# A mixture-of-experts kernel: turns of the next expert's first rows moved from the closing down products into the last block's up products

## The chip, the cores and the metric

The kernel runs on one core of a Trainium2 chip. The metric is the device time of one execution in microseconds (us). The time before is the median of 3 runs.

## The reference

The input x is two sequences of 2048 rows of 512 numbers (4096 tokens). It goes through a gated cross attention (16 heads, keys and values from a context of 128 rows each) and then through a gated mixture of experts, which is the stage that the change touches:

```python
xf = layernorm(x).reshape(4096, 512)
top_v, top_i = top_k(xf @ router_w.T, 2)          # two of 8 experts per token
C = ceil(4096 * 2 * 1.25 / 8)                     # 1280 slots per expert
slot = where(pos < C, experts * C + pos, E * C)   # each token's place with its expert
xb = buf.at[slot].set(xf[tokens])[:E * C].reshape(8, C, 512)
g, u = split(einsum('ecd,efd->ecf', xb, w12), 2)  # d_ff 2048
yb = einsum('ecf,edf->ecd', silu(g) * u, w3)
out = zeros.at[tokens].add(yb[slot] * weights)
x = x + tanh(g_ffn) * out
```

## The kernel before, in words

The first stage (up to about 540 us of the span) does attention, layer norm and routing, and writes each token's row to its slot in a DRAM buffer, `expert_rows`. The second stage goes over the 8 experts, one after the other, in a loop of its own on each engine (`experts`, L1240 to L1287).

**Tiles and blocks.** An expert has up to 10 tiles of 128 slots. How many it needs (nt) is read from the counts at run time, and the program has one body of code for each nt from 3 to 10. `pick` (L1268) compares and branches (L1273) to the body, and L1263 goes back to the top of the loop. `BLOCKS` cuts the tiles into blocks: 10 is (4, 3, 3), 9 is (3, 3, 3), 7 is (4, 3), 5 is (3, 2), 3 is (3,). In this data the experts have 9, 10, 10, 7, 10, 9, 5 and 3 tiles, called e0 to e7 below.

**Chunks.** The hidden width of 2048 is cut into 8 chunks of 256. For a chunk, each block is taken in turn: two steps j, each with a gate product G (bank `GB`) and an up product U (bank `UB`), each of 12 matmuls (4 pieces of the depth, and 3 passes for high and low parts of a split fp32 value, `passes`, L1536 to L1542). ScalarE takes silu of G (L1404), VectorE multiplies with U into `h32` (L1500), ScalarE rounds it to `h_hi` (L1410), and VectorE makes `h_lo` (L1506). The down products (`g2`, L1604) run one block behind: 6 matmuls of 512 columns for each tile, added into `yacc` by VectorE (`add`, L1466 to L1481). Beside these, each chunk splits the next chunk's weights in 6 units: `w_high` on ScalarE (L1368) and `w_low` on VectorE (L1443).

**Turns.** The rows of an expert arrive with the slots in the partitions and must be turned. A turn (`turn`, L1544) is 4 transposes by TensorE into one of the two banks `XBK`, then a copy of the high part by ScalarE (`x_high`, L1370 to L1373, tile `slotsT_hi`) and a subtraction by VectorE (`x_low`, L1446 to L1450, tile `slotsT_lo`). The two banks take turns, so that turn i waits for `x_low` of turn i - 2. The first `XA` = 4 tiles of an expert are turned at the end of the expert before it, and the others during its own first chunk (`slots_at`).

**The closing.** In an expert's last chunk the down products of the last two blocks are not followed by another block of the expert. They run in an order written out by `closing` (L1218), which all three engines follow: turn 0, turn 1, y0, y1, turn 2, y2, turn 3, y3 and the rest, where y is a down product. Their results go to the banks that `closing_bank` names. A down product on a `YB` bank that was used before in the same closing waits until that bank's result has been added (L1648). After the closing ScalarE has also scaled each tile (`scaled`, L1392) for the scatter by GpSimd.

```python
order, downs = [("x", 0), ("x", 1)], len(closing_downs(nt))
for i in range(downs):
    order.append(("y", i))
    if 1 <= i <= XA - 2:
        order.append(("x", i + 1))
```

Each engine works through its instructions in the order written. Nothing is reordered by a scheduler, so the place of a call in this code is its place in the engine's queue.

Of the kernel before, what the change touches and what calls it, by code (L numbers as in the profile page):

```python
# [5 lines left out]
def flamingo_gated_layer(  # L6
# [64 lines left out]
    with ExitStack() as whole:  # L71
# [1046 lines left out]
        with ExitStack() as stage:  # L1118
# [94 lines left out]
            def closing_bank(nt, i):  # L1213

                from_end = len(closing_downs(nt)) - 1 - i
                return [UB[1], GB[1], UB[0], GB[0], YB[1], YB[0], YB[1], YB[0]][from_end]

            def closing(nt):  # L1218


                order, downs = [("x", 0), ("x", 1)], len(closing_downs(nt))
                for i in range(downs):
                    order.append(("y", i))
                    if 1 <= i <= XA - 2:
                        order.append(("x", i + 1))
                return order

            def by_tiles(eng, n_e, body):
                def pick(sizes):
# [63 lines left out]
            with nc.Block(no_gpsimd_drain=True) as block:  # L1293
# [71 lines left out]
                def _(act):  # L1365
# [4 lines left out]
                    def x_high(i, tp, at, done):  # L1370
                        act.wait_ge(tp, at)
                        nc.scalar.copy(xT_hi[:, :, i * P:(i + 1) * P],  # L1372
                                       XBK[i % 2][:, :].rearrange("p (k t) -> p k t", k=KD)).then_inc(done, 1)  # L1373
# [6 lines left out]
                    def chunk(nt, e, c, par, half, first, last):  # L1380
                        base, tiles = steps_before(e, c), tiles_before(e, c)
                        loads = e * (NCH // 2) + half + 1

                        def units(which):
                            for i in which:
                                if i == 0:
                                    act.wait_ge(raw_loaded[1 - par], 16 * loads)
                                if i == NU12 and not first:

                                    act.wait_ge(y_ready, tiles)  # L1390
                                w_high(1 - par, i)

                        def scaled(t):

                            act.wait_ge(y_added, downs_done(nt, tiles, t))
                            nc.scalar.activation(yout[:, t, :], yacc[:, t, :], ACT.Copy,  # L1396
                                                 scale=wslot[:, t:t + 1]).then_inc(yout_ready, tile_of(nt, t))

                        for b, width in enumerate(BLOCKS[nt]):
                            W = width * P  # L1400
                            for j in range(NJ):
                                q = NJ * b + j
                                act.wait_ge(g_ready, base + q + 1)
                                nc.scalar.activation(silu[q % 2][:, 0:W], GB[q % 2][:, 0:W], ACT.Silu)\  # L1404
                                  .then_inc(silu_ready, step_of(nt, q))
                                if first:
                                    for i in slots_at(nt, q, 0):
                                        x_high(i, xb_tp, XB * e + i - XA + 1, xb_hi)
                                act.wait_ge(h32_ready, base + q + 1)
                                nc.scalar.copy(h_hi[h_buf(nt, par, b)][:, j, 0:W], h32[q % 2][:, 0:W])\  # L1410
                                  .then_inc(hhi_ready, step_of(nt, q))
                                if first:
                                    for i in slots_at(nt, q, 1):
                                        x_high(i, xb_tp, XB * e + i - XA + 1, xb_hi)
                                units(units_at(nt, q))
                            if last and b == 0:
                                act.wait_ge(weights_ready, e + 1)
                                act.wait_ge(yout_free, e + 1)
                            if last and 0 < b < len(BLOCKS[nt]) - 1:
                                for t in block_tiles(nt, b - 1):  # L1420
                                    scaled(t)
                        if not last:
                            units(late_units(nt))
                        if first and nt < NT:
                            act.sem_inc(xb_tp, min(XB, NT - nt))
                        if last:
                            for kind, i in closing(nt):
                                if kind == "x":
                                    x_high(i, xa_tp, XA * (e + 1) + i + 1, xa_hi)
                                    continue  # L1430
                                t, earlier = closing_downs(nt)[i]
                                if not earlier:
                                    scaled(t)
                            units(late_units(nt))
# [4 lines left out]
                def _(dve):  # L1439
# [17 lines left out]
                    def chunk(nt, e, c, par, half, first, last):  # L1457
# [25 lines left out]
                        for b, width in enumerate(BLOCKS[nt]):  # L1483
# [9 lines left out]
                            for j in range(NJ):  # L1493
                                q = NJ * b + j
                                if first:
                                    for i in slots_at(nt, q, 0):
                                        x_low(i, xb_hi, XB * e + i - XA + 1, xb_lo)
                                dve.wait_ge(silu_ready, base + q + 1)
                                dve.wait_ge(u_ready, base + q + 1)
                                nc.vector.tensor_tensor(h32[q % 2][:, 0:W], silu[q % 2][:, 0:W], UB[q % 2][:, 0:W], ALU.mult)\  # L1500
# [8 lines left out]
                                if first:  # L1509
                                    for i in slots_at(nt, q, 1):  # L1510
                                        x_low(i, xb_hi, XB * e + i - XA + 1, xb_lo)
                                units(units_at(nt, q))
                            for t in downs[1:]:
                                add(t, at, opens)
# [20 lines left out]
                def _(pe):  # L1535
# [22 lines left out]
                    def chunk(nt, e, c, par, half, first, last):  # L1558
# [3 lines left out]
                        def rest_of_slots(q, half_of):  # L1562
                            for i in slots_at(nt, q, half_of):
# [3 lines left out]
                                    pe.wait_ge(xb_lo, XB * e + i - XA - 1)  # L1567
                                turn(i, xb_tp)

                        def g1(b):  # L1570
                            W = BLOCKS[nt][b] * P
                            cols = slice(first_tile(nt, b) * P, first_tile(nt, b + 1) * P)
# [9 lines left out]
                            for j in range(NJ):  # L1582
# [8 lines left out]
                                passes(GB[q % 2][:, 0:W], list(zip(stat(j), moving))).then_inc(g_ready, step_of(nt, q))  # L1591
                                if first:
                                    rest_of_slots(q, 0)
                                if q >= 2:
                                    pe.wait_ge(h32_ready, base + q - 1)
                                elif not first:
                                    pe.wait_ge(h32_ready, base)
                                else:
                                    pe.wait_ge(y_added, Y0 + tiles - 2 + 2 * q)
                                passes(UB[q % 2][:, 0:W], list(zip(stat(NJ + j), moving))).then_inc(u_ready, step_of(nt, q))  # L1600
                                if first:
                                    rest_of_slots(q, 1)

                        def g2(t, b, earlier, y=None):  # L1604

# [27 lines left out]
                        if last:  # L1633
                            downs = closing_downs(nt)
                            banks = [closing_bank(nt, i) for i in range(len(downs))]
                            for kind, i in closing(nt):
                                if kind == "x":
                                    if i % 2 == 0:
                                        pe.wait_ge(xrow_loaded[i // 2], 16 * (e + 2))
                                    if i >= 2:  # L1640
                                        pe.wait_ge(xa_lo, XA * (e + 1) + i - 1)
                                    turn(i, xa_tp)
                                    continue
                                t, earlier = downs[i]
                                at = tiles_before(e, c - 1) if earlier else tiles
# [52 lines left out]
```

## Time and profile before

| | |
|---|---|
| median of 3 runs | 2720.58 us (2719.67 to 2720.8) |
| the profiled execution | 2716.51 us |
| its span | 2714.1 us |
| TensorE busy | 2608.7 us, 96% of the span |
| VectorE busy | 1392.1 us, 51% |
| ScalarE busy | 944.7 us, 35% |
| GpSimd busy | 410.9 us, 15% |
| mean granted TensorE clock | 0.984 |

The profiled execution's own time is its span and 2.4 us around it. In the rows, PE is TensorE (PEld its weight loads), DVE is VectorE, ACT is ScalarE, POOL is GpSimd and SP is the engine that issues the loads; a q behind an engine's name is its sequencer. A matmul's recorded length is longer than the distance to the next one, because matmuls overlap, so the distance between starts is what a matmul costs. Expert e1 begins at about 856 us, e2 at 1195, e3 at 1535, e4 at 1773, e5 at 2110, e6 at 2418 and e7 at 2593.

### The profile page before, as it was taken

How to read it: one execution, taken by the hardware profiler on the slowest of the kernel's cores; microseconds unless marked ns; L12 is line 12 of the kernel's file. 1: busy time of each engine (PE TensorE's matmuls, PEld its weight loads, DVE VectorE, ACT ScalarE, POOL GpSimd, SP SyncE). 2: the span in 40 equal slices, each digit the busy share in tenths (PEclk: the TensorE clock that was granted, in tenths of full speed). 3: DMA queues.
4: the chain of work that ended last, by engine and by line, in shares of the span. 5: the costliest groups of instructions: out<-in, count | busy, mean ns of one | idle time of the engine just before them, and what ended most of it. 6: DMA issues, size and time to landing. Idle time of an engine off the chain costs nothing.

```text
span 2714.1 us, 40566 instructions
## 1 busy us (share of the span) xinstructions
PE 2608.7 (96%) x14166; PEld 2313.9 (85%) x14167; DVE 1392.1 (51%) x2647; ACT 944.7 (35%) x2479; POOL 410.9 (15%) x391
## 2 busy tenths in 40 slices
PE   5999999589999999999999999999999999999988
PEld 4877777489998888888988888888889999989987
DVE  4788888544444444444444444444444444445555
ACT  4766666222224222242222322232222322233343
POOL 2455555400002000020000300010000100030030
PEclk8999999799999999999999999999999999999999
DMA  7523222321103201132011321141011311033142
GB/s 266 213 78 102 94 78 97 122 111 47 46 27 77 86 24 46 47 62 86 23 46 46 63 109 46 47 113 40 30 46 39 107 47 46 33 85 118 70 126 81
DMA packets 60034, 208.38 MB, mean 77 GB/s; under 512 B 9564, under 2 KB 9836, under 8 KB 51602
## 3 DMA queue, kind: packets, MB, share of 16 engines
q1 hardware_dynamic: 43282, 175.30, 18.0%
q0 software_dynamic: 16640, 31.69, 6.1%
q8 instruction: 59, 0.97, 0.1%
q14 instruction: 53, 0.43, 0.1%
HBM read 145.60 MB, written 67.70 MB: 79 GB/s over the span
## 4 chain that ended last, share of the span: by engine, by line
PE 76%; issue 2%; DVE 1%; ACT 1%; DVEq 0%; DMA 0%; ACTq 0%; POOL 0%; POOLq 0%
PE bank L1540 75%; PE bank L1546 1%; DVE yacc L1480 1%; DVE slotsT_lo L1449 0%; ACT slotsT_hi L1372 0%; DVE h L1500 0%; DMA xrow<-expert_rows 0%; ACT later_hi L1368 0%; ACT yout L1396 0%; ACT h_hi L1410 0%; POOL out_dram L1354 0%; DVE w_lo L1443 0%; DVEq L1252 0%; ACT silu L1404 0%; DVEq L1479 0%
## 5 line engine op out<-in xcount | busy, mean ns | idle before, releaser
L1500 DVE TENSOR_TENSOR h<-silu,bank 128x384 f32<-128x384 f32 (+2 forms) x320 | 183.8, 574 | 826.3 <-PE bank L1540 816.8
L1540 PE MATMUL bank<-slotsT_hi,early_hi 128*128 128x384 f32 (+2 forms) x1280 | 444.6, 347 | 14.4 <-issue 12.3
L1540 PE MATMUL bank<-slotsT_hi,w_hi 128*128 128x384 f32 (+2 forms) x1280 | 442.5, 346 | 5.3 <-DVE w_lo L1443 5.3
L1540 PE MATMUL bank<-slotsT_lo,early_hi 128*128 128x384 f32 (+2 forms) x1280 | 442.5, 346 | 0.4 <-issue 0.4
L1540 PE MATMUL bank<-slotsT_lo,w_hi 128*128 128x384 f32 (+2 forms) x1280 | 442.2, 345 | 0.0
L1540 PE MATMUL bank<-slotsT_hi,early_lo 128*128 128x384 f32 (+2 forms) x1280 | 441.8, 345 | 0.0
L1540 PE MATMUL bank<-slotsT_hi,w_lo 128*128 128x384 f32 (+2 forms) x1280 | 441.1, 345 | 0.0
L1410 ACT CAST h_hi<-h 128x384 fp32r<-128x384 f32 (+2 forms) x320 | 169.2, 529 | 745.9 <-DVE h L1500 743.0
L1404 ACT ACTIVATE silu<-bank 128x384 f32<-128x384 f32 (+2 forms) x320 | 162.0, 506 | 728.8 <-PE bank L1540 728.3
L1480 DVE TENSOR_TENSOR yacc<-bank,yacc 128x512 f32<-128x512 f32 x464 | 316.6, 688 | 169.0 <-PE bank L1540 169.0
L1540 PE MATMUL bank<-later_hi,h_hi 128*128 128x512 f32 x1008 | 399.8, 397 | 0.3 <-DVE yacc L1480 0.3
L1540 PE MATMUL bank<-later_lo,h_hi 128*128 128x512 f32 x1008 | 398.7, 396 | 0.0
L1540 PE MATMUL bank<-later_hi,h_lo 128*128 128x512 f32 x1008 | 398.3, 395 | 0.0
L1354 POOL DMA_INDIRECT out_dram<-yout,token x63 | 97.9, 1554 | 1973.9 <-ACT yout L1396 1962.4
L1540 PEld LDWEIGHTS bank<-slotsT_hi,early_hi 128*128 128x128 f32 x1280 | 241.6, 189 | 30.2 <-issue 13.6
L1540 PEld LDWEIGHTS bank<-slotsT_hi,w_hi 128*128 128x128 f32 x1280 | 241.3, 189 | 20.5 <-DVE w_lo L1443 6.1
L1540 PEld LDWEIGHTS bank<-slotsT_lo,early_hi 128*128 128x128 f32 x1280 | 241.7, 189 | 13.1 <-issue 0.8
L1540 PEld LDWEIGHTS bank<-slotsT_lo,w_hi 128*128 128x128 f32 x1280 | 241.4, 189 | 12.6
L1540 PEld LDWEIGHTS bank<-slotsT_hi,early_lo 128*128 128x128 f32 x1280 | 241.6, 189 | 10.7
L1540 PEld LDWEIGHTS bank<-slotsT_hi,w_lo 128*128 128x128 f32 x1280 | 241.4, 189 | 10.8
L1506 DVE TENSOR_TENSOR h_lo<-h,h_hi 128x384 fp32r<-128x384 f32 (+2 forms) x320 | 183.8, 574 | 105.4 <-ACT h_hi L1410 104.8
L1540 PEld LDWEIGHTS bank<-later_hi,h_lo 128*128 128x128 f32 x1008 | 189.3, 188 | 44.9
(195 smaller groups left out, 3533.3 us busy)
## 6 DMA issues: line engine op xcount, KB each, us to landing
staged<-in_moe_w_dram SPq DMA_DIRECT2D x33, 1536.0 KB
raw<-in_moe_w_dram SPq DMA_DIRECT2D x32, 1536.0 KB, 6.4
xrow<-expert_rows SPq DMA_DIRECT2D x42, 520.0 KB, 9.0
expert_rows<-zeros SPq DMA_DIRECT2D x40, 520.0 KB, 7.5
xin<-in_x_dram SPq DMA_DIRECT2D x17, 512.0 KB, 3.7
xres<-in_x_dram SPq DMA_DIRECT2D x15, 512.0 KB, 3.7
out_dram<-xres SPq DMA_DIRECT2D x15, 512.0 KB
staged<-in_L_xattn_Wq_dram SPq DMA_DIRECT2D x1, 1024.0 KB, 10.7
```

The costliest lines, as they stand in the source:

```text
L1354: nc.gpsimd.indirect_dma_start(out=out_tok, out_offset=bass.IndirectOffsetOnAxis(ap=token[:, i:i + 1], axis=0), in_=yout[:, i, :] if t < n ...
L1404: nc.scalar.activation(silu[q % 2][:, 0:W], GB[q % 2][:, 0:W], ACT.Silu)\
L1410: nc.scalar.copy(h_hi[h_buf(nt, par, b)][:, j, 0:W], h32[q % 2][:, 0:W])\
L1480: nc.vector.tensor_tensor(yacc[:, t, :], y[:, :], yacc[:, t, :], ALU.add)\
L1500: nc.vector.tensor_tensor(h32[q % 2][:, 0:W], silu[q % 2][:, 0:W], UB[q % 2][:, 0:W], ALU.mult)\
L1506: nc.vector.tensor_tensor(h_lo[hb][:, j, 0:W], h32[q % 2][:, 0:W], h_hi[hb][:, j, 0:W].bitcast(fp32), ALU.subtract)\
L1540: last = nc.tensor.matmul(out_ap, st, mv, start=(at == 0), stop=(at == n - 1))
L1546: last = nc.tensor.transpose(XBK[i % 2][:, k * P:(k + 1) * P], xrow[:, i, k * P:(k + 1) * P], ident[:, :])
```

## The change

`next_slots_at` puts turn i of the next expert's first rows into the last block of the last chunk: turn 0 behind the first gate product, turn 1 behind the first up product, turn 2 behind the second gate product, turn 3 behind the second up product. A turn is only moved there when its tile of the slots' buffer belongs to an earlier block, whose products have read it by then. For nt of 7 or more all 4 turns move, for nt = 5 three of them (turn 3 stays, now ahead of the closing's first down product), and for nt = 3 none. On ScalarE and VectorE the copies and subtractions move in the same way, and `closing` keeps only what is left.

```diff
+            def next_slots_at(nt, q, half):
+                last = len(BLOCKS[nt]) - 1
+                i = 2 * (q - NJ * last) + half
+                return [i] if 0 <= i < min(XA, first_tile(nt, last)) else []
+
             def closing(nt):
-                order, downs = [("x", 0), ("x", 1)], len(closing_downs(nt))
-                for i in range(downs):
-                    order.append(("y", i))
-                    if 1 <= i <= XA - 2:
-                        order.append(("x", i + 1))
-                return order
+                turns = [("x", i) for i in range(min(XA, first_tile(nt, len(BLOCKS[nt]) - 1)), XA)]
+                downs = [("y", i) for i in range(len(closing_downs(nt)))]
+                return turns[:2] + downs[:2] + turns[2:3] + downs[2:3] + turns[3:] + downs[3:]
...
                                 nc.scalar.activation(silu[q % 2][:, 0:W], GB[q % 2][:, 0:W], ACT.Silu)\
...
+                                if last:
+                                    for i in next_slots_at(nt, q, 0):
+                                        x_high(i, xa_tp, XA * (e + 1) + i + 1, xa_hi)
                                 act.wait_ge(h32_ready, base + q + 1)
                                 nc.scalar.copy(h_hi[h_buf(nt, par, b)][:, j, 0:W], h32[q % 2][:, 0:W])\
...
+                                if last:
+                                    for i in next_slots_at(nt, q, 1):
+                                        x_high(i, xa_tp, XA * (e + 1) + i + 1, xa_hi)
                                 units(units_at(nt, q))
...
+                                if last:
+                                    for i in next_slots_at(nt, q, 0):
+                                        x_low(i, xa_hi, XA * (e + 1) + i + 1, xa_lo)
                                 dve.wait_ge(silu_ready, base + q + 1)
                                 dve.wait_ge(u_ready, base + q + 1)
...
+                                if last:
+                                    for i in next_slots_at(nt, q, 1):
+                                        x_low(i, xa_hi, XA * (e + 1) + i + 1, xa_lo)
                                 units(units_at(nt, q))
...
+                        def next_slots(i):
+                            if i % 2 == 0:
+                                pe.wait_ge(xrow_loaded[i // 2], 16 * (e + 2))
+                            if i >= 2:
+                                pe.wait_ge(xa_lo, XA * (e + 1) + i - 1)
+                            turn(i, xa_tp)
...
                                 passes(GB[q % 2][:, 0:W], list(zip(stat(j), moving))).then_inc(g_ready, step_of(nt, q))
...
+                                if last:
+                                    for i in next_slots_at(nt, q, 0):
+                                        next_slots(i)
...
                                 passes(UB[q % 2][:, 0:W], list(zip(stat(NJ + j), moving))).then_inc(u_ready, step_of(nt, q))
...
+                                if last:
+                                    for i in next_slots_at(nt, q, 1):
+                                        next_slots(i)
```

**VectorE, nt = 10, the last block of the last chunk and the start of the closing.** In these rows bank6 and bank7 are the turns' banks, h32 and h_lo belong to the block's second step, later_lo is a unit of the next weights, and yacc is an add. Before:

```order
L1500 TENSOR_TENSOR h32_1<-silu1,bank3 128x384
L1506 TENSOR_TENSOR h_lo1<-h32_1,h_hi1 128x384
L1442 REGISTER_ALU
L1443 TENSOR_TENSOR later_lo<-staged,later_hi 128x512
L1447 ISA
L1449 TENSOR_TENSOR slotsT_lo<-bank6,slotsT_hi 128x4x128
L1447 REGISTER_ALU
L1449 TENSOR_TENSOR slotsT_lo<-bank7,slotsT_hi 128x4x128
L1469 REGISTER_ALU
L1480 TENSOR_TENSOR yacc<-bank4,yacc 128x512
```

And now:

```order
L1458 TENSOR_TENSOR slotsT_lo<-bank6,slotsT_hi 128x4x128
L1510 REGISTER_ALU
L1512 TENSOR_TENSOR h32_1<-silu1,bank3 128x384
L1518 TENSOR_TENSOR h_lo1<-h32_1,h_hi1 128x384
L1456 REGISTER_ALU
L1458 TENSOR_TENSOR slotsT_lo<-bank7,slotsT_hi 128x4x128
L1451 REGISTER_ALU
L1452 TENSOR_TENSOR later_lo<-staged,later_hi 128x512
L1478 REGISTER_ALU
L1489 TENSOR_TENSOR yacc<-bank4,yacc 128x512
```

One subtraction of a turn now stands ahead of the product h32, and one between h_lo and the weights' unit. Before, two stood behind the unit and ahead of the first add.

**TensorE, nt = 10, the last up product's end and the closing's start.** xrow are the rows that are turned, and later_hi and h_hi the operands of a down product. Before, two turns stood together between the up product and y0:

```order
L1540 MATMUL bank<-slotsT_lo,w_hi 128x384
L1540 MATMUL bank<-slotsT_hi,w_lo 128x384
L1639 ISA
L1546 MATMUL bank<-ident,xrow 128x128 x8
L1653 REGISTER_ALU
L1540 MATMUL bank<-later_hi,h_hi 128x512
```

And now one turn stands there, and one behind each of the three products before it, of which this is the second gate product's:

```order
L1555 MATMUL bank<-slotsT_hi,w_lo 128x384
L1589 REGISTER_ALU
L1561 MATMUL bank<-ident,xrow 128x128 x4
L1555 MATMUL bank<-slotsT_hi,w_hi 128x384
L1555 MATMUL bank<-slotsT_lo,w_hi 128x384
```

The closing's 36 matmuls of down products now follow each other with no turn between them.

## Rows read from the trace of the kernel before

**Rows 1.** The page: span, busy time and instructions, and the chain by line

```profile
span 2714.1 us, 40566 instructions
...
PE 2608.7 (96%) x14166; PEld 2313.9 (85%) x14167; DVE 1392.1 (51%) x2647; ACT 944.7 (35%) x2479; POOL 410.9 (15%) x391
...
PE bank L1540 75%; PE bank L1546 1%; DVE yacc L1480 1%; DVE slotsT_lo L1449 0%; ACT slotsT_hi L1372 0%; DVE h L1500 0%; DMA xrow<-expert_rows 0%; ACT later_hi L1368 0%; ACT yout L1396 0%; ACT h_hi L1410 0%; POOL out_dram L1354 0%; DVE w_lo L1443 0%; DVEq L1252 0%; ACT silu L1404 0%; DVEq L1479 0%
```

**Rows 2.** Waits of TensorE from 560 us to the end: total us, times, longest

```profile
PE bank L1540 <- issue: 5.6, 3, 2.7
PE bank L1540 <- DVE w_lo L1443: 5.3, 1, 5.3
PE bank L1540 <- DVE yacc L1480: 2.4, 2, 2.1
PE bank L1546 <- DVE slotsT_lo L1449: 1.2, 3, 0.7
```

**Rows 3.** Instructions that touch the tile xrow: ns min/median/max, first and last start

```profile
L1546 PE MATMUL bank<-ident,xrow x272: 270/272/477, 538.2 to 2700.0; 128*128 128x128 f32 x136
```

**Rows 4.** Timeline of TensorE at turns: start us, us, operation, idle before

```profile
564.27 0.60 PE L1546 MATMUL bank<-ident,xrow 128*128 128x128 f32 x4
564.63 0.42 PE L1540 MATMUL bank<-slotsT_hi,early_hi 128*128 128x384 f32 x1
...
1184.52 0.34 PE L1540 MATMUL bank<-slotsT_hi,w_lo 128*128 128x384 f32 x1
1184.70 1.04 PE L1546 MATMUL bank<-ident,xrow 128*128 128x128 f32 x8
1185.49 0.48 PE L1540 MATMUL bank<-later_hi,h_hi 128*128 128x512 f32 x1
```

**Rows 5.** Timeline of VectorE, e3, the last step and the closing's start

```profile
1761.05 0.55 DVE L1500 TENSOR_TENSOR h<-silu,bank 128x384 f32<-128x384 f32 x1 [1.24 <-PE bank L1540]
1762.31 0.56 DVE L1506 TENSOR_TENSOR h_lo<-h,h_hi 128x384 fp32r<-128x384 f32 x1 [0.70 <-ACT h_hi L1410]
1762.79 0.68 DVE L1443 TENSOR_TENSOR later_lo<-staged,later_hi 128x512 fp32r<-128x512 f32 x1
1763.39 1.28 DVE L1449 TENSOR_TENSOR slotsT_lo<-bank,slotsT_hi 128x512 fp32r<-128x512 f32 x2
1764.59 1.28 DVE L1480 TENSOR_TENSOR yacc<-bank,yacc 128x512 f32<-128x512 f32 x2
```

**Rows 6.** Timeline of ScalarE in the same stretch

```profile
1761.69 0.51 ACT L1410 CAST h_hi<-h 128x384 fp32r<-128x384 f32 x1 [2.27 <-DVE h L1500]
1762.11 0.62 ACT L1368 CAST later_hi<-staged 128x512 fp32r<-128x512 f32 x1
1762.63 1.06 ACT L1372 CAST slotsT_hi<-bank 128x512 fp32r<-128x512 f32 x2
```

**Rows 7.** Timeline of TensorE in the same closing: turn 2 and y2

```profile
1764.42 0.60 PE L1546 MATMUL bank<-ident,xrow 128*128 128x128 f32 x4
1765.32 0.50 PE L1540 MATMUL bank<-later_hi,h_hi 128*128 128x512 f32 x1 [0.31 <-DVE yacc L1480]
```

**Rows 8.** Timelines of three engines from e2's closing into e3

```profile
1531.80 1.88 DVE L1480 TENSOR_TENSOR yacc<-bank,yacc 128x512 f32<-128x512 f32 x3
...
1532.27 0.40 PE L1540 MATMUL bank<-later_hi,h_lo 128*128 128x512 f32 x1
...
1539.16 1.28 ACT L1404 ACT_TABLE_LOAD   x1 [4.70 <-issue]
...
1542.31 0.66 PE L1546 MATMUL bank<-ident,xrow 128*128 128x128 f32 x4 [0.28 <-DVE slotsT_lo L1449]
```

**Rows 9.** The branch to a body of code, TensorE's sequencer, 1529 to 1536 us

```profile
L1273 PEldq COMPARE_BRANCH  x5: 64/64/4982, 1529.5 to 1530.0; - x5
```

**Rows 10.** Timeline of VectorE at the start of e7

```profile
2601.22 0.56 DVE L1500 TENSOR_TENSOR h<-silu,bank 128x384 f32<-128x384 f32 x1 [8.38 <-issue]
```

**Rows 11.** Stretches: us, busy us (x) of each engine, granted clock, DMA share, GB/s

```profile
2608.00:2614.00 6.00, 6.00 (x24) 6.00 (x23) 1.64 (x2) 0.49 (x1) 4.78 (x4) 0.61 0.77 270
```

More of the change, by code:

```diff
@@ L1637, in chunk @@
                                 if kind == "x":
[L1638 to L1642, printed above, removed]
+                                    next_slots(i)
                                     continue
```

## The prediction

> **What bounds the kernel now.** I read the page first. TensorE is busy for 2608.7 of 2714.1 us, and its split products on one line hold 75% of the chain that ended last, while a turn's line holds 1% [rows 1]. So the first question for any edit is whether TensorE gets less work or loses a wait. The second view is TensorE's list of waits over the whole expert stage [rows 2]. From 560 us to the end it is idle for 5.6 + 5.3 + 2.4 + 1.2 = 14.5 us in 9 waits. That is all that a change of order in this stage could win, if TensorE's work stays the same. None of these rows names a turn's copy as what a down product waits for. Of the 2.4 us on yacc, 0.31 us is a wait inside a closing, that of e3 [rows 7]; the other 2.1 us falls on the start of e7.
>
> The issue row and most of that 2.1 us have another cause, which the sequencer shows. At the start of e3 the compare and branch to the body of code takes 4982 ns where the others take 64 [rows 9], and TensorE runs dry behind it. The wait has 3 occurrences of up to 2.7 us [rows 2], at e3, e6 and e7. The 5.3 us wait for w_lo comes from VectorE, which is idle for 8.38 us with no releaser at the start of e7 [rows 10].
>
> **The change part by part.**
>
> *The turns on TensorE.* There are 272 transposes in 68 turns [rows 3], and the change removes none. It moves 4 turns for each of e0 to e5 and 3 for e6, 27 in all; e7 has 3 tiles and keeps its order. The price is read from starts. Eight transposes ahead of a down product hold it up by 1185.49 - 1184.70 = 0.79 us, and four ahead of a 384-column product by 564.63 - 564.27 = 0.36 us [rows 4]. The difference, 0.43 us, is one turn. A matmul of 384 columns takes 1184.70 - 1184.52 = 0.18 us (0.34 us is its recorded length), so a product of 12 takes 2.1 us, and one of 512 columns in proportion 0.23 us, a down product of 6 thus 1.4 us. The 0.36 us was taken in the middle of a product sequence like the one that the turns move into, so a turn costs the same in either place. What differs is only the number of times that TensorE changes over: before, 3 groups of turns for an expert, now 4. I put that at nothing, with bounds of 0 and 0.1 us for each of 7 experts, by the few hundredths that are left between the two prices above. The 27 turns cost 27 x 0.43 = 11.6 us before, and 11.6 us after.
>
> *Do they hide in the new place?* They could only do so in idle time of TensorE, and the last block has none: rows 2 holds no wait on the G and U products inside an expert. Each product there needs nothing that comes late. So the 11.6 us stay on the path.
>
> *New waits of the turns.* Turn 2 needs the subtraction of turn 0 (the bank is the same). Turn 0's transposes follow the first G. ScalarE does silu beside them, then the copy (about 0.56 us each by the 1.06 us of a pair [rows 6]), and VectorE the subtraction (about 0.68 us, 1.28 us for a pair [rows 5]). That is done some 2.1 us after the first G. TensorE comes to turn 2 only after a turn, a U of 12 matmuls, another turn and a G, 5 us in all (0.43 + 2.1 + 0.43 + 2.1). Turn 3 needs turn 1's subtraction, which now stands behind h_lo. Counting from the start of h, h_lo ends at 1762.87 - 1761.05 = 1.82 us, the subtraction 0.6 to 0.7 us later, at 2.5 us [rows 5], against 4.5 us and more. Both waits cost nothing, with 2 us of cover. If the cover went, turn 2 or 3 would be late first, and the product behind it.
>
> *What is queued behind the waiting instruction.* On VectorE the subtraction of turn 0 now stands ahead of h for the same step. It is done 2.1 us after G, and U ends 2.5 us after G (0.43 + 2.08), so h is on time, by 0.4 us. If it were late, h_hi and h_lo would be late, and the first reader of the last block's h is y3, three down products later, at 1.4 us each. So this delay too is covered, by about 4 us less the 1.8 us of the chain.
>
> *The Trainium skill speaks against this order.* VectorE's order is that of the rows: after h it does h_lo, then the unit of weights, one behind the other [rows 5], and with the change the turn's subtraction is one more in the line. The Trainium skill, TensorE: Matmul & The Clock Gate, section "Architectural detail: the array is 16× 32×32, not 1× 128×128", says of VectorE and ScalarE that they are "strict FIFO". By that rule a turn that comes late holds up the block's own products, which is the rival on the slow side below. The trace agrees on the order and shows 0.4 us of room; by the rule with that room gone the sum would be the rival's +8.1 us, by the rows it is 0.
>
> *The closing of e3 (nt = 7).* This is the one closing with a wait. Its y2 goes to the bank of y0 and waits until y0 is added. Before, y2 could have started 0.36 us after turn 2, at 1764.78, and started at 1765.32: 0.54 us lost [rows 7]. Counted from h at 1761.05, y2 was wanted at 3.73. With the change only one turn lies between the last U and y0, not two, and none ahead of y2, so that it is wanted at 3.73 - 2 x 0.43 = 2.87. VectorE now does h_lo to 1.82, one subtraction to 2.43, the unit of weights to about 3.03 and then y0's add to about 3.65 (steps of some 0.6 us, since they overlap by 0.08 [rows 5]). ScalarE's copies are ahead of these (h_hi at 0.64, turn 3's copy to 1.62, the unit to 2.14 [rows 6]). So y2 starts at 3.70 and loses 0.83 us, 0.3 us more than before. With 10, 9 or 5 tiles no bank is used twice with a wait in the closing, and this term is 0.
>
> *The ends of the closings.* Before, turn 3's subtraction stands ahead of the adds of y3, y4 and y5, and these run in a row of 1.88 us from 1531.80, so that the last begins at 1533.00, while y5's matmuls end at 1532.27 + 0.40 = 1532.67 [rows 8]. With the turns gone the last add follows y5 at once, 0.3 us sooner. ScalarE's scaling and what it does next come 0.3 us sooner too. At e2 and e4 TensorE waits for none of this [rows 2], and at e1 for VectorE's branch, which starts with y5 and not with the add. At e3 and e5 the turns of the next expert's own rows wait for ScalarE's and VectorE's first work (0.28 us idle at e3 [rows 8], 0.7 us at e5, the longest of [rows 2]), and each gives back up to 0.3 us, if the branch's 4 us stay what they are. At e7 VectorE is late by the 8.38 us [rows 10] and would leave 0.2 us sooner. I take -0.3, -0.3 and -0.2 us.
>
> *Other queues.* The load of weights for the chunk after next waits for the last unit, which comes some 2 us later now (4 turns less 2, and one subtraction). At e7, where chunks are shortest, a chunk still lasts 4 x 2.1 + 3 x 1.4 = 12.6 us, against which 2 us is little. No DMA is added, and GpSimd has nothing moved. This is 0.
>
> **The sum.** 0 for the turns, +0.3 at e3's closing, -0.8 at the starts of e3, e5 and e7, and 0 to +0.7 for changing over, taken as +0.1: **-0.4 us**. The profiled execution took 2716.51 us, so the same execution would take 2716.1. The median of the runs is 4.07 us above the profiled one, and I carry the difference over to it: 2720.58 - 0.4 = **2720.2 us**.
>
> **The rivals.**
>
> *The turns hide after all (faster).* If they did, 27 x 0.43 = 11.6 us would go, and the time would be 2709. Only a TensorE that waits inside the last block could give that. Rows 2 speaks against it. Chance 0.02.
>
> *The turns block the block (slower).* In the last block's VectorE queue the subtraction of turn 0 is ahead of h. From the point where it ends over 0.4 us later than counted, h is late; when it ends 3 us later, turn 2 waits too, and TensorE with it. With 27 turns at 0.3 us, the size of the one wait for a subtraction in [rows 8], this gives 8.1 us, 2728. It would take a ScalarE held up by the adds and scaling of the block before. ScalarE is busy for 35% of the span. Chance 0.03.
>
> *The code lies otherwise (either side).* The long branches [rows 9, 10] are the largest idle times in the stage, and they are not on every expert. VectorE's 8.38 us at e7 is made of two of them, 4.2 us each. If one more falls on an expert, or one goes, TensorE gains or loses about 4 us, and the clock with it. The clock's price: after the wait at e7 the granted clock is 0.61 over 6 us [rows 11], which is 4.7 us at 1.2 GHz in place of 2.4, and costs 2.3 us. Together 6.5 us, so 2713.7 or 2726.7. Against it stands that ScalarE and VectorE have the same number of rows in the new order and TensorE 7 more register operations in all. Chance 0.02 on either side. The Trainium skill, Runtime: NRT & Kernel Launch, section "Instruction fetch mechanics", says that a branch whose target is outside the fetched window of code stalls until it is fetched. By that rule a body that moved across a block's edge would change which branches stall. The trace agrees that a few branches are long and the rest are not; it does not show where the edges are.
>
> **How the numbers follow.** The forecast keeps 0.91. A measurement of this kernel tells 0.2%, 5.4 us, from no change, so the forecast is within 0.2%. Faster: 0.02 + 0.02 = 0.04. Slower: 0.03 + 0.02 = 0.05. Same: 0.91. For the range, the three starts at e3, e6 and e7 have TensorE idle for 2.1 to 2.7 us, and the clock fell after one of them and not after the others. The fall costs about 2.3 us and can come or go with a shift of less than a microsecond. One such change, and the bounds of the terms (-0.8 to +1.0), give 2717 to 2723.6. A second change of the clock would be 2.3 us further; I take half of that on the low side and little on the high side, 2716 to 2724.
>
> **What would show it.** In the changed kernel's profile TensorE's instructions and busy time should be the same to 1 us. In e2's closing six down products should follow each other with no turn between, 0.36 us behind the last turn's first transpose. y2 of e3's closing should wait about 0.8 us. No turn in a last block should show a wait. VectorE's adds of y3 to y5 should stand apart. The long branches should stand at the same experts, at 4 to 5 us. I am wrong if TensorE's waits in [rows 2] differ by more than 3 us in total, or if the last block shows a wait.

## The result and the profile after

The changed kernel's median is 2722.65 us (2715.86 to 2729.23, 18 runs), against 2717.64 us (2714.29 to 2720.8, 18 runs) of the kernel before, run beside it. The ratio is 1.0017, with a 95% interval of 1.0011 to 1.0024, which is 4.7 us slower (the medians are 5.0 us apart). Forecast were -0.4 us and 2720.2 us. The time lies in the range (2716 to 2724) and the change is within 0.2%, but its sign and size are not those of the sum. The profiled execution took 2719.85 us, before 2716.51 us.

Page of the changed kernel, span and engines:

```profile
span 2717.4 us, 40566 instructions
PE 2613.0 (96%) x14166; PEld 2322.4 (85%) x14167; DVE 1402.2 (52%) x2647; ACT 948.8 (35%) x2479; POOL 412.7 (15%) x391
```

The instructions are as many as before. TensorE's busy time is up by 4.3 us with the same matmuls. TensorE's waits from 560 us to the end, against [rows 2] (wait, sum in us, times, longest):

```profile
PE bank L1555 <- issue: 11.4, 4, 4.5
PE bank L1555 <- DVE w_lo L1452: 3.2, 1, 3.2
PE bank L1561 <- DVE slotsT_lo L1458: 1.1, 2, 0.6
PE bank L1555 <- DVE yacc L1489: 0.6, 1, 0.6
```

These are 16.3 us against 14.5. The row that grew is "issue", from 5.6 to 11.4 us. To place it, I took from the trace the start of the first matmul of each expert:

| from the start of | before, us | after, us | difference |
|---|---|---|---|
| e0 to e1 | 306.65 | 306.30 | -0.35 |
| e1 to e2 | 338.31 | 338.57 | +0.26 |
| e2 to e3 | 340.50 | 341.14 | +0.64 |
| e3 to e4 | 237.50 | 238.87 | +1.37 |
| e4 to e5 | 337.69 | 337.66 | -0.03 |
| e5 to e6 | 308.11 | 310.09 | +1.98 |
| e6 to e7 | 174.58 | 176.40 | +1.82 |
| e7 to the end | 120.86 | 118.76 | -2.10 |
| sum | 2164.2 | 2167.8 | +3.6 |

Four turns moved in each of e0 to e5. Where no long branch follows (e0, e1 and e4) the lengths differ by -0.35, +0.26 and -0.03 us: the turns cost the same in their new place. The loss is at the starts of e3, e6 and e7, and the compare and branch of TensorE's sequencer shows it (count, then min/median/max ns):

```profile
L1276 PEldq COMPARE_BRANCH  x5: 64/64/5672, 1529.1 to 1529.6; - x5
L1276 PEldq COMPARE_BRANCH  x3: 64/73/6925, 2414.7 to 2415.0; - x3
L1276 PEldq COMPARE_BRANCH  x1: 5922/5922/5922, 2592.4 to 2592.4; - x1
```

Before, [rows 9] had 4982 ns at e3, and at e6 and e7:

```profile
L1273 PEldq COMPARE_BRANCH  x3: 64/69/4922, 2413.1 to 2413.4; - x3
L1273 PEldq COMPARE_BRANCH  x1: 4337/4337/4337, 2588.5 to 2588.5; - x1
```

The same three branches are long, and each is longer than before, by 0.7, 2.0 and 1.6 us. There is a fourth one ahead of e0, of 6.1 us before and 6.0 us after, and one of 0.34 us at e5 in both. Before, at e0 and at e5:

```profile
L1273 PEldq COMPARE_BRANCH  x7: 64/64/6105, 542.6 to 543.4; - x7
L1273 PEldq COMPARE_BRANCH  x7: 64/64/337, 2107.6 to 2108.3; - x7
```

In the code, a compare whose branch isn't taken goes on to the next compare, and a taken branch leads to the body of its nt. Five are taken in this data. Four of them enter a body for the first time (e0 with 9 tiles, e3, e6 and e7), and these are the long ones. The fifth, at e5, goes back to the body with 9 tiles and takes 0.34 us. At e1, e2 and e4 (10 tiles) none is taken, and a compare that isn't taken took 64 to 84 ns in both traces.

What stands beside the three is the load of weights (1.5 MB) that SP issues when the chunk's last unit is split. SP's timeline at e6, after and then before:

```profile
2412.15 0.33 SPq L1301 DMA_DIRECT2D staged<-in_moe_w_dram  x1
```

```profile
2408.68 0.33 SPq L1298 DMA_DIRECT2D staged<-in_moe_w_dram  x1
```

Before, the load was issued 4.70 us ahead of the long branch, and now 2.84 us. At e3 this lead went from 4.87 to 2.94 us and at e7 from 3.78 to 1.89: 1.9 us less at each. The DMA queues in the first 2.7 us of e6's long branch (packets, MB, share of 16 engines). Before, the load (q1) is nearly over and two packets of instructions (q8) have gone through:

```profile
q0 software_dynamic: 122, 0.24, 69.8%
q1 hardware_dynamic: 34, 0.22, 19.5%
q8 instruction: 2, 0.03, 4.3%
```

After, the load fills the DMA engines and there is no packet of instructions; two come in the next 2.7 us:

```profile
q1 hardware_dynamic: 85, 0.97, 93.5%
q0 software_dynamic: 7, 0.01, 3.0%
```

```profile
q0 software_dynamic: 247, 0.46, 108.4%
q8 instruction: 2, 0.03, 7.8%
```

The length of a branch follows the packets of instructions. At e3 the one packet in it starts 2.65 us into the branch before and 3.34 us after. In 35 of the 36 branches at e3, e6 and e7 in all twelve kernels of this document, the branch ends 1.3 to 1.7 us after its last packet of instructions has ended (b_early2's at e3: 0.7 us). So a branch is as long as it takes until this packet has landed.

The theory that the experiments had to test was this: the change delays the load, the load meets the fetch of the next body's code, and the fetch takes longer. Its rivals were that the turns themselves hold something up in the new place, and that the code lies otherwise in memory.

### The profile page after: what moved, and what is told of

It reads as the page before. It is cut to its first block, busy times and chain, and to the rows that moved or that the text cites. A ratio compares the mean times of both kernels' runs of the same rounds, so it can differ in the third digit from the quotient of the medians.

```text
span 2717.4 us, 40566 instructions
## 1 busy us (share of the span) xinstructions
PE 2613.0 (96%) x14166; PEld 2322.4 (85%) x14167; DVE 1402.2 (52%) x2647; ACT 948.8 (35%) x2479; POOL 412.7 (15%) x391
## 4 chain that ended last, share of the span: by engine, by line
PE 78%; issue 1%; DVE 0%; ACT 0%; DMA 0%; DVEq 0%; POOL 0%; ACTq 0%; POOLq 0%
PE bank L1555 77%; PE bank L1561 1%; DVE yacc L1489 0%; DVE slotsT_lo L1458 0%; DMA xrow<-expert_rows 0%; DVE h L1512 0%; ACT slotsT_hi L1375 0%; POOL out_dram L1357 0%; ACT h_hi L1416 0%; DVE w_lo L1452 0%; DVEq L1255 0%; DVE early_lo L1452 0%; ACT yout L1399 0%; ACTq L1255 0%; ACT silu L1407 0%
## 5 line engine op out<-in xcount | busy, mean ns | idle before, releaser
L1555 PEld LDWEIGHTS bank<-slotsT_lo,w_hi 128*128 128x128 f32 x1280 | 241.2, 188 | 12.7
L1555 PEld LDWEIGHTS bank<-later_hi,h_hi 128*128 128x128 f32 x1008 | 189.3, 188 | 45.6 <-DVE yacc L1489 5.1
```

What stands on the lines that cost most here:

```text
L1555: last = nc.tensor.matmul(out_ap, st, mv, start=(at == 0), stop=(at == n - 1))
```

## The experiments

Ratios are against the kernel before, run in the same job. The stage is the distance from e0's first matmul to the end of the span, in the profiled execution; it leaves out the first stage, which differs from execution to execution. The ratios are taken over the executions and are not the quotients of the medians. Stages and lengths of branches come from one profiled execution of each kernel, which isn't always near its median: b_late2's took 2727.59 us against a median of 2723.43.

### The load alone, 1.2 us later

The kernel before, with no turn moved. SP's load at chunk 0 also waits for the subtraction of the second turn, in the loop and in the last expert's part:

```diff
                             sp.wait_ge(w_lo, units_before(e, c + 1))
+                            if c == 0:
+                                sp.wait_ge(xa_lo, XA * e + 2)
                             load_weights(e + (c + 2) // NCH, (c + 2) % NCH, c % 2)
```

> The kernel before, with one more wait on the engine that issues loads: the weights for the chunk after next are asked for only when turn 1's subtraction is done, in the closing, some 1.3 us later. No turn moves. Theory (the later load delays the fetch of code): the branches into the bodies of e3, e6 and e7 take 0.5 to 1.5 us longer each, and the time is 1 to 5 us above the kernel before. Rival (the turns in their new place cost): nothing changes, within 0.5 us.

Measured: 2723.43 us, ratio 1.0019 [1.0010, 1.0028], stage 2170.8 us. The load's lead over the long branch is 3.67, 3.51 and 2.49 us at e3, e6 and e7, 1.2 to 1.3 us less than before.

```profile
L1273 PEldq COMPARE_BRANCH  x5: 64/64/5767, 1533.9 to 1534.4; - x5
L1273 PEldq COMPARE_BRANCH  x3: 64/69/6940, 2419.4 to 2419.6; - x3
```

```profile
PE bank L1544 <- issue: 12.5, 4, 4.5
```

At e7 the branch takes 6.08 us. The delay alone gives the changed kernel's branches (5.67, 6.93 and 5.92 us there), its wait (11.4 us there) and its loss (1.0017 there). It doesn't take a moved turn. It does so with a delay of 1.2 us, where the change's is 1.9: the effect is not in proportion to the delay. At e3 the packet of instructions starts 3.44 us into the branch.

### The load alone, 4.4 us later

The same edit with `XA * e + 3`, so that SP waits for the third turn's subtraction.

> The kernel before with the load of weights asked for only when turn 2's subtraction is done, some 4 us later than before and three times as late as with the wait for turn 1. No turn moves. Theory: the load falls whole on the branches of TensorE and on those of VectorE and ScalarE, which come 3 us later; the time is 6 to 12 us above the kernel before. Rival (a later load costs only what it costs at 1.3 us, or nothing): 0 to 5 us.

Measured: 2731.77 us, ratio 1.0052 [1.0038, 1.0066], 14 us over the kernel before beside it, stage 2179.8 us. The lead is 0.46 and 0.37 us at e3 and e6, and at e7 the load is issued 0.67 us behind the branch's start. More delay costs more, and more than I had put.

```profile
L1273 PEldq COMPARE_BRANCH  x5: 64/64/7092, 1534.6 to 1535.1; - x5
L1273 PEldq COMPARE_BRANCH  x3: 64/69/6603, 2421.4 to 2421.7; - x3
L1273 PEldq COMPARE_BRANCH  x1: 3842/3842/3842, 2603.3 to 2603.3; - x1
```

```profile
PE bank L1544 <- issue: 11.6, 4, 4.8
PE bank L1544 <- DVE w_lo L1447: 8.7, 1, 8.7
```

The branches did not grow as a whole. At e7 TensorE's was shorter and it was VectorE that came later: TensorE's wait for its w_lo rose from 5.3 to 8.7 us. At e1, where TensorE has no long branch, its wait for VectorE's first subtraction also rose, from 0.28 to 2.58 us, behind 7.23 us in which VectorE waits for nothing that the trace names, and e1 became 3.6 us longer. I take this for a load that is late enough to miss one engine's fetch and to meet another's; the traces don't name the engine that a packet of instructions is for, so this is argued and not shown.

### The load held until after the branches, in both orders

SP waits for the first unit of the next expert, which is split behind the branches. This goes into the kernel before (b_held) and into the changed one (a_held):

```diff
-                            sp.wait_ge(w_lo, units_before(e, c + 1))
+                            sp.wait_ge(w_lo, units_before(e, c + 1) + (1 if c == 0 else 0))
```

The order of before with the load held:

> The kernel before, with that load held until the next expert's first unit of weights is split, when all engines have reached their new body. Theory: with no load beside them the long branches of TensorE fall from 4.3 to 5.0 us to 3 us or less, and the time is 3 to 8 us below the kernel before. Rival: the branches stay at 4 to 5 us and the time within 0.5 us, or the load comes late at e7 and it is slower.

Measured: 2719.96 us, ratio 0.9999 [0.9990, 1.0009], stage 2163.6 us.

```profile
L1273 PEldq COMPARE_BRANCH  x5: 64/64/5177, 1528.9 to 1529.4; - x5
L1273 PEldq COMPARE_BRANCH  x3: 64/69/4941, 2412.3 to 2412.6; - x3
```

The order of after with the load held:

> The changed kernel with the same hold. Theory: the two orders then take the same time to 0.7 us, since the fetch is no longer behind the load; so 3 to 8 us below the kernel before. Rival (the turns cost in their new place): it stays 3 to 5 us above the kernel before with the same hold.

Measured: 2715.41 us, ratio 0.9997 [0.9987, 1.0006], stage 2162.5 us.

```profile
L1276 PEldq COMPARE_BRANCH  x5: 64/64/3367, 1530.9 to 1531.4; - x5
L1276 PEldq COMPARE_BRANCH  x3: 64/69/3682, 2414.3 to 2414.5; - x3
```

With the load out of the way the moved turns' loss is gone, which speaks against both rivals: the turns stand where they stood in the change. The two orders are not told apart: the intervals overlap, the medians are 4.6 us apart in favour of the changed order, and the executions of either spread over 8 us. But against the kernel before nothing was gained, where the theory had put 3 to 8 us. In b_held the branches at e3 and e6 stay at 5 us with no load beside them. GpSimd's scatters (q0) are there instead. In b_held their packets start 0.47 and 0.63 us into these two branches, and the last packet of instructions at 2.85 and 2.58 us. In a_held they start at 1.15 and 1.32 us, behind that packet, which comes at 1.00 and 0.99 us, and the branches take 3.4 and 3.7 us. So the moved turns also shift the scatters against the branch. VectorE is still late at e7 (w_lo, 6.4 us in b_held and 5.8 us in a_held).

### The last units earlier, in both orders

Instead of holding the load, let it go sooner: in the last chunk the last units move up by one step j, so that the load is issued earlier relative to the branch.

```diff
-            def units_at(nt, q):
+            def units_at(nt, q, last=False):
 
                 plan = {1: ((0, 1), (2, 3)), 2: ((0,), (1, 2), (3, 4), (5,)), 3: ((0,), (1,), (2,), (3,), (4,), (5,))}
+                if last:
+                    plan.update({2: ((0,), (1, 2), (3, 4, 5), ()), 3: ((0,), (1,), (2,), (3,), (4, 5), ())})
                 return plan[len(BLOCKS[nt])][q]
...
-                                units(units_at(nt, q))
+                                units(units_at(nt, q, last))
```

In the changed kernel:

> The changed kernel with the last unit of the next weights split one step earlier in an expert's last chunk, so that the load is asked for some 4 us sooner and has nearly ended when the branch begins. Theory: the branches are down to 4 us or less, and the time is 0 to 5 us below the kernel before. Rival: as the changed kernel, 4 to 5 us above the kernel before.

Measured: 2718.26 us, ratio 1.0005 [0.9996, 1.0014], stage 2161.1 us, branches 4.35, 4.43 and 4.18 us, where I had put 4 or less. In the kernel before (another job):

> The kernel before with the last unit of the next weights split one step earlier in an expert's last chunk, so that the load is asked for some 4 us sooner. Theory: the branches take 4.4 us or less at e3 and e6, and the time is 0 to 4 us below the kernel before and the same as the changed kernel with this edit, to 1 us. Rival (the turns in their new place cost): it is 3 us or more below the changed kernel with this edit.

Measured: 2714.93 us, ratio 0.9993 [0.9984, 1.0002], stage 2162.2 us.

```profile
L1275 PEldq COMPARE_BRANCH  x5: 64/64/4272, 1529.5 to 1530.0; - x5
L1275 PEldq COMPARE_BRANCH  x3: 64/69/3943, 2412.5 to 2412.7; - x3
```

With an earlier load the branches are shorter than before's in both orders, by 0.2 to 1.0 us, and the change's loss is no longer to be seen. Neither kernel is told from before by its time.

### Without the scatters, and without either

What the branch costs when nothing else is on the DMA engines. Both kernels leave out adding the experts' results to the output. The first does so alone:

```diff
-                                nc.gpsimd.indirect_dma_start(
...
-                                    bounds_check=T - 1, oob_is_err=False, compute_op=ALU.add).then_inc(added, 16)
+                                pool.sem_inc(added, 16)
```

> The kernel before without its scatters: the results of the experts are not added to the output in DRAM. The load of weights stays. The scatters are the other traffic beside the fetch. Theory: a branch that has only the load beside it takes as long as the load still runs, plus the fetch itself, so 2.5 to 4 us. Rival (the fetch time has nothing to do with DMA traffic): 4.3 to 5.0 us as before.

Measured, one run: 2703.14 us, stage 2151.5 us, branches 3.96, 4.70 and 3.97 us. The one at e6 is in the range of the rival (4.3 to 5.0) and not of the theory (2.5 to 4). The second also holds the load, as above:

> The kernel before without the scatters (results not added to the output) and with the load held until the next expert's first unit. Nothing else is on the DMA engines at the branch. Theory: the bare fetch, 1.5 to 2.5 us, so that TensorE hardly runs dry at e3, e6 and e7, and its waits for issue go to under 1 us. Rival: branches of 4 us and more.

Measured, one run: 2703.89 us, stage 2151.9 us, and the issue wait is down to 1.2 us.

```profile
L1273 PEldq COMPARE_BRANCH  x5: 64/64/3557, 1529.1 to 1529.6; - x5
L1273 PEldq COMPARE_BRANCH  x3: 64/69/3721, 2411.3 to 2411.6; - x3
L1273 PEldq COMPARE_BRANCH  x1: 3740/3740/3740, 2584.9 to 2584.9; - x1
```

```profile
PE bank L1537 <- issue: 1.2, 1, 1.2
```

A long branch costs 3.6 to 3.7 us with the DMA engines free; I had put 1.5 to 2.5. What is over that, 0.6 to 1.4 us before and 2.1 to 3.2 us after, I put down to transfers beside it. Most of the 13 us that both gain isn't the branches: 9.0 of the 12.7 us by which b_noscat's stage is shorter lie behind e7's start. They were not followed further, since these kernels lack a part of the work.

### The last units two steps earlier, in both orders

With three blocks, units 3, 4 and 5 all at step 3: `3: ((0,), (1,), (2,), (3, 4, 5), (), ())`, the rest as above. In the kernel before:

> The kernel before with the last three units of the next weights split together two steps earlier in the last chunk of the experts with 9 or 10 tiles (7 and 5 tiles as in the edit of one step). Theory: the load is over before the branch at e3, and the time is 0 to 4 us below the kernel before, as with one step. Rival: the three units in one step hold up VectorE and TensorE waits in the last block, slower than with one step.

Measured: 2718.73 us, ratio 1.0008 [0.9999, 1.0016], stage 2165.3 us. In the changed one:

> The changed kernel with the same edit, on the same chip as the one without the turns moved. Theory (the turns themselves cost nothing in either place): the two are the same to 1 us. Rival (the turns cost in the last block, hidden so far by the gain on the load): this one is 3 us or more above its partner.

Measured: 2721.93 us, ratio 1.0012 [1.0004, 1.0021], stage 2165.8 us. The branches are short (4.51, 4.28 and 3.32 us; 4.72, 4.38 and 3.96 us), but new waits take their place. In b_early2 TensorE's down products at 1175.88, 1514.71 and 2093.97 us wait about 1 us each for an add that stands behind the three units; the first of them:

```profile
1175.88 0.50 PE L1542 MATMUL bank<-later_hi,h_hi 128*128 128x512 f32 x1 [0.95 <-DVE yacc L1482]
```

The stages of the two orders differ by 0.6 us. The medians differ by 3.2 us, which is the size that I had put for the rival (the turns cost in the last block), but the intervals overlap, and with the load held the medians differed the other way. The two orders are not told apart here either; each interval reaches some 2.4 us to either side, and a difference of that size could hide in them. Against the kernel before, a_early2 is slower beyond its interval. The profiled a_early2 has a first stage 5.5 us longer than b_early2's, an execution's own difference.

## Why the prediction was right and wrong

**The step that failed** is the one headed "Other queues": "The load of weights for the chunk after next waits for the last unit, which comes some 2 us later now" was right, by 1.9 us, and "This is 0" was wrong. I asked whether the weights would still be there in time, and they were. I did not ask what the load meets on the DMA engines while it runs. It meets the fetch of the next body's code, and with 1.9 us less lead the fetch comes later (the last packet of instructions starts 0.7 us later in the branch at e3, 0.6 us at e6, where it also takes 2.1 us in place of 0.95, and 1.6 us at e7). The sum relied on "if the branch's 4 us stay what they are"; they became 5.7, 6.9 and 5.9 us. The lead is not the whole rule: b_late2's 3.51 us at e6 gave 6.94 us, and before's 3.78 us at e7 gave 4.34.

**Where the 3.6 us of the profiled execution went.** The gap at the start, over the usual distance of two products, grew at e3 from 2.86 to 3.50 us, at e6 from 2.62 to 4.65 and at e7 from 2.22 to 3.26, 3.7 us together. Behind the gap the granted clock fell. The stretch of 4 us behind e3's start, after and then before (PEclk is third from the right):

```profile
1536.00:1540.00 4.00, 4.00 (x12) 3.17 (x11) 0.00 (x0) 1.28 (x1) 3.09 (x2) 0.57 1.04 152
```

```profile
1536.00:1540.00 4.00, 4.00 (x23) 3.39 (x22) 0.00 (x0) 0.84 (x1) 3.09 (x2) 1.00 1.02 140
```

Seven matmuls after stand 0.427 us apart and the others 0.233 us, which costs 1.4 us and is the table's e3 row; matmuls at half the rate are also in TensorE's busy time. The rows at e6, after and then before, show the fall there in both:

```profile
2422.00:2428.00 6.00, 5.25 (x18) 4.65 (x19) 0.00 (x0) 1.86 (x3) 2.69 (x2) 0.55 0.88 131
```

```profile
2418.40:2424.40 6.00, 5.30 (x23) 4.95 (x24) 0.00 (x0) 2.25 (x3) 3.86 (x3) 0.73 0.98 142
```

By (0.73 - 0.55) x 6 this is 1.1 us more. Against these stands e7's wait for VectorE, 3.2 us where it was 5.3: TensorE itself comes later, and waits less for an engine that is as late as before. That gives 2.1 us back. Together 3.7 + 1.4 + 1.1 - 2.1 = 4.1 us, against the 3.6 us measured.

**The turns: right.** No turn and no product waits in a last block, and among the products of 384 columns the next matmul starts 1178.46 - 1178.11 = 0.35 us behind a turn's start, as [rows 4] had it:

```profile
1177.93 0.34 PE L1555 MATMUL bank<-slotsT_hi,w_lo 128*128 128x384 f32 x1
1178.11 0.60 PE L1561 MATMUL bank<-ident,xrow 128*128 128x128 f32 x4
1178.46 0.43 PE L1555 MATMUL bank<-slotsT_hi,w_hi 128*128 128x384 f32 x1
```

The prediction priced a turn at 0.43 us and left open what the few hundredths between its two prices (0.36 and 0.43) meant. The traces show it: the first matmul behind a group of turns stands 0.26 us from its next one where 0.175 is usual (0.32 and 0.23 with 512 columns). So a lone turn costs 0.35 + 0.09 = 0.44 us and a pair 0.79 + 0.09 = 0.88, and the 0 to 0.7 us that the sum allowed for changing over is 0.

**e3's closing: right in kind.** y2 waits longer, by 0.2 us where 0.3 was forecast (0.74 against 0.83 us lost):

```profile
1766.45 0.40 PE L1555 MATMUL bank<-later_hi,h_lo 128*128 128x512 f32 x1
1767.42 0.50 PE L1555 MATMUL bank<-later_hi,h_hi 128*128 128x512 f32 x1 [0.57 <-DVE yacc L1489]
```

**The ends of the closings: the mechanism right, the gain partly missed.** VectorE's adds now stand apart, where [rows 8] had three in a row; the last two:

```profile
1530.96 0.69 DVE L1489 TENSOR_TENSOR yacc<-bank,yacc 128x512 f32<-128x512 f32 x1 [0.71 <-PE bank L1555]
1532.36 0.69 DVE L1489 TENSOR_TENSOR yacc<-bank,yacc 128x512 f32<-128x512 f32 x1 [0.71 <-PE bank L1555]
```

The wait of e3's first own turn is gone (0.45 us before, by the turn's start), but e5's stayed (0.82 and 0.78 us) and e1's grew (0.45 to 0.69). Why e5's stayed is open.

**The rivals.** "The turns hide" and "the turns block the block" did not come. "The code lies otherwise" looked at the right place, the long branches, with a wrong mechanism: the same three branches are long, and it is their length that changed. b_late2 changes it with no turn moved.

**The signs.** "The long branches should stand at the same experts, at 4 to 5 us" was the sign that spoke: the experts were the same, and the lengths were 5.7, 6.9 and 5.9 us. TensorE's instructions were as said, its busy time was not (4.3 us more, where 1 was allowed). The waits differ by 1.8 us in total, under my 3 us mark, because one rose by 5.8 and others fell: a total over all waits was too coarse a sign.

The Trainium skill, Runtime: NRT & Kernel Launch, section "Instruction fetch mechanics", says that a taken branch to code outside what has been fetched makes the engine wait for a DMA of that code. The traces agree that the code comes over the DMA engines (q8's packets in the long branches) and that only taken branches are long; the 0.34 us at e5 is a taken one that is not. Beside other transfers such a packet starts later: at e6 the first one starts 0.75 us into the branch before and 2.84 us into it after.

## What to carry to other kernels

A step that is moved ahead of a trigger moves the transfer that the trigger starts, even when the step itself costs nothing. Ask what that transfer then runs beside, the fetch of code behind a run-time branch included, and not only whether its data come in time. To settle such a case, shift the transfer alone, with the order of the work untouched, then take the transfer away with the order changed.

## What the hardware showed that I had not expected

- A taken branch that enters its body for the first time holds TensorE's sequencer for 3.6 to 3.7 us with the DMA engines free, 3.3 to 5.2 us beside scatters, and up to 7.1 us beside a load of 1.5 MB. The branch back to a body that has run took 0.34 us.
- When it begins, TensorE still has 10 to 12 matmuls to start at e3, e6 and e7, before and after. In the kernel before the last of them starts 2.2 to 2.4 us into the branch, so that the 4.98 us at e3 leave TensorE idle for 2.7 us.
- With the DMA engines free the last packet of instructions starts 0.9 to 1.25 us into the branch, and at e6 the first of the two starts 0.45 us ahead of it. In the kernel before it starts at 1.9 to 2.7 us, and in the changed one at 3.1 to 3.5.
- Where the two packets at e6 run side by side, the second takes 2.05 to 2.09 us (the changed kernel, b_late2, b_noscat), and 0.94 to 1.3 us in the nine others.
- A later load doesn't only cost more and more on one engine: at 4 us it missed TensorE's fetch at e7 (3.84 us) and VectorE's lateness took over (8.7 us).

Still open: why the branch back to a body that has run is short, what besides the lead and the scatters sets the length of the others, and whether earlier units in the order of before (0.9993 [0.9984, 1.0002]) are worth anything. No version was shown to be faster than the kernel before.
